# Second expert layer of a graph and mixture-of-experts kernel: groups of 128 tokens by unordered pairs of experts

## The chip, the cores and the metric

The kernel runs on one core of one Trainium2 chip. The metric is the device time in microseconds (us) of that core; the kernel before took 976.24 us, the median of three runs (975.2 to 976.76). A core has a matrix engine (PE, with its weight loads shown as PEld), VectorE (DVE), ScalarE (ACT), GpSimd (POOL) and SyncE (SP), each with a queue of its own, and 16 DMA engines that all of them share. Engines are ordered among each other by semaphores only.

## The reference, cut to what matters

128 graphs of 64 nodes with 128 features give 8192 tokens. The result is built in four residual steps: attention, experts, attention, experts.

```python
x = x + gnn0(layernorm(x), adj)
x = x + ffn0(layernorm(x))        # 8 experts, hidden width 512, best 2 of 8, weights renormalised
x = x + gnn1(layernorm(x), adj)
x = x + ffn1(layernorm(x))        # 8 experts, hidden width 256, best 2 of 8, weights = softmax values
```

Only ffn1 is touched in earnest. For each token with normalised row xf it is

```python
probs = softmax(xf @ gate_w + gate_b)
top2_vals, top2_idx = top_k(probs, 2)
out = sum over the two experts e of  val_e * (gelu(xf @ W1[e] + b1[e]) @ W2[e] + b2[e])
```

## The kernel before, in words

The program is five stages, one after the other, with all engines in each: blocks of layer 0 (attention and routing), groups of layer 0 (experts), blocks of layer 1, groups of layer 1, and a last stage that adds the results.

**Blocks.** `blocks(L)` takes 8 blocks of 1024 tokens, as 8 tiles of 128. Per block VectorE brings in the input (in layer 1 it adds the two expert results of layer 0, L932), takes statistics (L877), makes the masked scores, adds the attention to the input (`add_attention`, L984) into `x1w`, finds the two best experts (`route`) and computes for every token and expert the row in a sorted buffer (`places`, L1038 to L1053). PE does the transposes, the scores, features and attention, and the running counts (`ranks`, L535 to L540). PE's L506 writes half the partitions at a time with a 64-column weight tile; all its other operations use 128 by 128 tiles. POOL then scatters each token's row twice, once to each of its experts, into `row_buf` (L446): 16 indirect DMAs of 128 rows of 130 floats per block. SP stores the attention result with the two weights into `x1_buf` (L300).

A row is the normalised token as a high and a low half in f16, its token number and its expert's number. `row_buf` has a region for each expert; `pad_row` fills what isn't used, a fixed part of it in layer 0's blocks (L355) and the ends of the regions once the counts are known (L368).

**Groups.** `groups(L)` runs over 71 groups of 256 sorted rows, each of one expert (`NG = 16384 / 256 + 7`), in turns of 8. `group_tables` makes the list of the groups' experts and rows. SP loads the rows four groups ahead (L378). PE transposes them (L593), multiplies them by the first weights, three f16 products for each f32 one (`up`, L607), and after ACT's gelu, which adds the first bias, and VectorE's split into a high and a low half (L1184, L1188) by the second weights (`down`, L621). VectorE adds the second bias (L1201) and computes the destination (L1173, L1176, L1198), POOL scatters 2 times 128 result rows of 128 floats into `y_buf` (L454). On PE, group g's transposes come three groups ahead, its first product two groups ahead of its second one. PE reads the experts' numbers of a turn into registers at its start.

**The last stage.** SP loads `x1_buf` and both halves of `y_buf` back, VectorE adds the two weighted results to each token (L932, 128 instructions), SP writes the output (L429).

## Time and profile before

| what | value |
|---|---|
| median of three runs | 976.24 us |
| the profiled execution's own time | 975.38 us |
| its span, first to last instruction | 973.5 us |
| time around the span | 1.88 us |
| busy, share of the span: PE, PEld, DVE, ACT, POOL | 66%, 56%, 77%, 49%, 56% |
| granted clock of TensorE, mean over the span | 0.789 of 2.4 GHz |
| indirect DMAs of POOL | 256 into row_buf, 284 into y_buf |

Busy shares are means over five stages with different limits, so they name no bound by themselves. The stages are told apart by which lines run: layer 0's blocks to about 209 us, its groups from 244 to 470 us, layer 1's blocks to 702 us, its groups from 732 to 928 us, and the last stage to 973.5 us. An idle time in a row is the wait of that engine just before the instruction, with what ended it.

### The profile page before, as it was taken

Reading aid. Unit: us, or ns where it says so; the run is one execution under the profiler, and the core shown is the slowest. Engines: PE = TensorE matmul, PEld = TensorE weight load, DVE = VectorE, ACT = ScalarE, POOL = GpSimd, SP = SyncE. Lnnn points to the kernel's source line nnn. Section 1 sums busy time; section 2 is a strip of 40 time slices with the busy share of each in tenths; the row PEclk is TensorE's granted clock in tenths of the full one; section 3 lists DMA queues with packets and bytes.
Section 4 is the critical chain, followed back from the end, with each engine's and each line's share of the span. In section 5 each row is a group of like instructions: output and inputs, shape, how many; then the busy total and the mean of one; then the engine's idle time right before and its main releaser. Section 6 shows DMA issues by size and latency. Waiting matters only on the chain.

```text
span 973.5 us, 23618 instructions
## 1 busy us (share of the span) xinstructions
PE 641.5 (66%) x6081; PEld 547.3 (56%) x6082; DVE 752.1 (77%) x2881; ACT 480.3 (49%) x1065; POOL 545.7 (56%) x544
## 2 busy tenths in 40 slices
PE   3767667550999999999077768777207777777400
PEld 2656556450899999998056557655206655555300
DVE  6688898763699999999468989997526778787458
ACT  2365665420677777776046655665205655555100
POOL 0017677676276776767200665666763777777700
PEclk9875775755899999999557776777558999999655
DMA  8283333232233332326524454332333333333899
GB/s 221 61 199 107 112 93 95 69 107 77 71 88 89 88 87 82 86 82 176 140 57 120 137 146 136 88 88 66 94 90 87 105 98 102 94 104 97 226 233 285
DMA packets 168828, 111.51 MB, mean 115 GB/s; under 512 B 30306, under 2 KB 157737, under 8 KB 168776
## 3 DMA queue, kind: packets, MB, share of 16 engines
q1 hardware_dynamic: 151496, 77.04, 30.7%
q0 software_dynamic: 17280, 33.87, 10.4%
q8 instruction: 21, 0.34, 0.1%
q14 instruction: 31, 0.25, 0.1%
HBM read 60.32 MB, written 52.36 MB: 116 GB/s over the span
## 4 chain that ended last, share of the span: by engine, by line
PE 34%; DVE 22%; issue 19%; POOL 13%; DMA 5%; ACT 5%; SPq 1%; POOLq 1%; DVEq 0%; ACTq 0%
PE bank L607 10%; PE bank L621 9%; POOL row_buf L446 7%; POOL y_buf L454 5%; PE bank L509 4%; DVE xin L932 3%; PE bank L490 3%; DVE stat L877 3%; DVE x1w L984 3%; PE bank L506 2%; ACT xn L682 2%; PE bank L526 2%; PE bank L593 2%; DMA y_buf<-g_y,g_dst 2%; PE bank L513 2%
## 5 line engine op out<-in xcount | busy, mean ns | idle before, releaser
L446 POOL DMA_INDIRECT row_buf<-pay,slot x256 | 253.8, 992 | 245.0 <-DVE slot L1053 165.7
L454 POOL DMA_INDIRECT y_buf<-g_y,g_dst x284 | 291.6, 1027 | 137.0 <-issue 89.0
L607 PE MATMUL bank<-g_xT,w 128*128 128x256 f16 x1278 | 168.1, 278 | 0.9 <-ACT g_xT L786 0.3
L786 ACT ACTIVATE g_xT<-bank 128x512 f16<-128x512 f16 x142 | 84.8, 598 | 168.5 <-PE bank L593 164.4
L607 PEld LDWEIGHTS bank<-g_xT,w 128*128 x1278 | 118.3, 99 | 19.6 <-issue 2.1
L593 PE MATMUL bank<-ident,g_in 128*128 128x128 f16 x568 | 57.3, 225 | 83.6 <-DMA g_in<-row_buf 70.0
L793 ACT ACTIVATE xn<-bank,b_cols 128x256 f32<-128x256 f32 x216 | 86.8, 474 | 23.0 <-PE bank L607 15.9
L621 PE MATMUL bank<-w,g_h 128*128 x1260 | 84.4, 219 | 18.6 <-DVE g_y L1201 18.6
L793 ACT ACTIVATE xt<-bank,b_cols 128x256 f32<-128x256 f32 x210 | 84.5, 474 | 14.6 <-PE bank L607 11.4
L621 PEld LDWEIGHTS bank<-w,g_h 128*128 128x128 f16 x1260 | 76.0, 98 | 27.2 <-issue 25.1
L593 PEld LDWEIGHTS bank<-ident,g_in 128*128 128x128 f16 x568 | 37.0, 100 | 93.2 <-issue 73.9
L1173 DVE TENSOR_SCALAR g_k<-g_in,grp_e 128x2 f32<-128x2 f32 x142 | 34.1, 240 | 43.9 <-DMA g_in<-row_buf 36.0
L682 ACT ACTIVATE xn<-xin,nmr,rstd 128x128 f32<-128x128 f32 x128 | 50.8, 480 | 31.4 <-DVE nmr L921 31.4
L932 DVE SCALAR_TENSOR_TENSOR xin<-yin,xin 128x128 f32<-128x128 f32 x160 | 43.7, 345 | 26.7 <-DMA yin<-y_buf 24.2
L509 PEld LDWEIGHTS bank<-to_score,xnT 128*128 128x128 f32 x256 | 49.6, 289 | 22.3 <-issue 22.3
L490 PE MATMUL bank<-cst,xn 128*128 128x128 f32 x128 | 31.9, 412 | 44.1 <-ACT xn L682 41.4
L1201 DVE SCALAR_TENSOR_TENSOR g_y<-bank,b_bc 128x256 f32<-128x256 f32 x142 | 59.5, 419 | 0.0
L509 PE MATMUL bank<-to_score,xnT 128*128 128x64 f32 x256 | 55.1, 385 | 0.0
L526 PE MATMUL bank<-h_sb,pair_eT 128*128 128x137 f32 (+1 forms) x256 | 52.2, 384 | 2.4 <-ACT pair_eT L672 2.4
L526 PEld LDWEIGHTS bank<-h_sb,pair_eT 128*128 128x128 f32 x256 | 49.1, 288 | 6.4 <-issue 4.0
L1198 DVE CAST g_dst<-g_row 128x2 uint32<-128x2 f32 x142 | 25.9, 182 | 33.4 <-DMA y_buf<-g_y,g_dst 33.1
L490 PEld LDWEIGHTS bank<-cst,xn 128*128 128x128 f32 x128 | 22.4, 208 | 48.3 <-ACT xn L682 37.6
(182 smaller groups left out, 1333.7 us busy)
## 6 DMA issues: line engine op xcount, KB each, us to landing
g_in<-row_buf SPq DMA_DIRECT2D x142, 130.0 KB
yin<-y_buf SPq DMA_DIRECT2D x24, 512.0 KB, 6.2
x_buf<-x1w SPq DMA_DIRECT2D x16, 520.0 KB, 4.6
xin<-x_buf SPq DMA_DIRECT2D x10, 520.0 KB, 4.4
y_buf<-g_y,g_dst POOLq DMA_INDIRECT x284
xin<-in_x_dram SPq DMA_DIRECT2D x8, 512.0 KB, 4.2
adj_in<-in_adj_dram SPq DMA_DIRECT2D x16, 256.0 KB, 3.2
row_buf<-pay,slot POOLq DMA_INDIRECT x256, 2.4
```

The lines of the kernel that those rows point to most:

```text
L446: pool.indirect_dma_start(row_buf[L][:, :], bass.IndirectOffsetOnAxis(ap=slot[q][:, k, t:t + 1], axis=0), pay[q][:, t, :], None).then_inc( ...
L454: pool.indirect_dma_start(y_buf[L][:, :], bass.IndirectOffsetOnAxis(ap=g_dst[k][:, t:t + 1], axis=0), g_y[k][:, t, :], None, bounds_check= ...
L490: last = nc.tensor.transpose(bank[t // 4][:, (t % 4) * P:(t % 4 + 1) * P], src[:, t, :], ident)
L509: last = nc.tensor.matmul(bank[2][:, t * NODES:(t + 1) * NODES], xnT[:, t, :], to_score[:, 2 * L, :], start=False, stop=(t % 4 == 3), skip ...
L526: last = nc.tensor.matmul(att_tile[L][t], pair_eT[:, t, :], h_sb[:, t, H_AT:H_AT + att_w[L]], start=True, stop=True)
L593: last = nc.tensor.transpose(x_ps[q][:, hl, t * P:(t + 1) * P], rows16[:, t, hl * D:(hl + 1) * D], ident16[:, :])
L607: last = nc.tensor.matmul(dst, w[:, bass.ds(e * (2 * HID[L]) + (wp * HID[L] + c * P), P)], g_xT[q][:, xp, :], start=(m == 0), stop=(m == 2))
L621: last = nc.tensor.matmul(bank[5 + k % 2][:, t * D:(t + 1) * D], hid[:, hp, c, t * P:(t + 1) * P], w[:, bass.ds(e * (2 * HID[L]) + (2 * c ...
L682: last = nc.scalar.activation(dst[:, t, :], src[:, t, :], ACT.Identity, bias=nmr[:, t:t + 1], scale=rstd[:, t:t + 1])
L786: nc.scalar.activation(g_xT[q][:, :, :], x_ps[q], ACT.Copy).then_inc(s.gT_sb, 1)
L793: nc.scalar.activation(g_act[q][:, c, :], bank[2 * q + c // 2][:, (c % 2) * GRP:(c % 2 + 1) * GRP], ACT.Gelu, bias=b1_cols[L][:, bass.ds(e ...
L932: last = V.scalar_tensor_tensor(src[:, t, X_AT:X_END], y[k][:, t, :], src[:, t, k:k + 1], src[:, t, X_AT:X_END], ALU.mult, ALU.add)
```

## The change

Layer 1's experts are no longer taken one by one. There are 28 unordered pairs of experts; every token belongs to one pair.

- **Routing.** `route_pairs` makes a key from the two experts (a power of two for each, added) and compares it with the 28 keys; `ranks` and `places_pairs` count in 28 lists instead of 8. The weights are put in the pair's order. Each token is scattered once, as a row of 260 floats: the former 130, and beside them the attention result with its weights (`row0`, `row1` hold both side by side). Layer 1 has no store to an `x1_buf` any more; the reuse of `x1w` waits for the scatter of two blocks before instead.
- **Pads.** 128 pad rows of 260 floats ahead of each of the 28 lists are written once in layer 0's blocks. The last group of a list starts 128 rows before its end; rows that this takes twice get a destination out of bounds (`twice`). The writes to the ends of the regions are gone.
- **Tables.** `pair_tables` makes the pair's two experts, the first row and the count of rows taken twice for 91 groups (`NGP = 8192 / 128 + 27`) on partitions, and PE spreads them with one product. `pair_constants` prepares constants and bias rows on VectorE between `split_first(0)` and `groups(0)`.
- **Groups.** `pair_groups` runs over 91 groups of 128 rows, two experts each, in turns of 8, rows loaded eight groups ahead. PE does 2 transposes, 16 products in `up` (for each of 2 experts and 2 chunks three f16 products and one that adds the first bias) and 14 in `down` (for each expert one for the second bias and six). The bias products have 2 rows on the contracted side (`b1_row`, `sx_row`, `b2_row`, `sh_row` are tiles of 2 partitions), all others 128. ACT does one gelu over 512 columns and the high half after it, VectorE the low half and two multiply-adds with the token's weights, the second onto the attention result. POOL scatters 128 finished rows straight to the output.
- **The last stage** is gone, and with it the second `y_buf` and `x1_buf`.

The core of the diff:

```diff
+                def up(g, k, es):
+
+                    wait_past(pe, s.act_done, g - 3)
+                    pe.wait_ge(s.gT_sb, g + 1)
+                    w = w1[1][:, :, :, :].rearrange("p e a h -> p (e a h)")
+                    for m, e in enumerate(es):
+                        for c in range(NC[1]):
+                            dst = bank[k % 4][:, (m * NC[1] + c) * PG:(m * NC[1] + c + 1) * PG]
+                            for j, (wp, xp) in enumerate(((0, 0), (0, 1), (1, 0))):
+                                nc.tensor.matmul(dst, w[:, bass.ds(e * (2 * HID[1]) + (wp * HID[1] + c * P), P)],
+                                                 p_xT[k % 2][:, xp, :], start=(j == 0), stop=False)
+                            last = nc.tensor.matmul(dst, b1_row[:, bass.ds(e * HID[1] + c * P, P)], sx_row[:, :], start=False, stop=True)
+                    last.then_inc(s.h_ps, 1)
+
+                def down(g, k, es):
+                    w = w2[1][:, :, :, :, :].rearrange("p e c a d -> p (e c a d)")
+                    wait_past(pe, s.y_ready, g - 1)
+                    hid = p_h[k % AHEAD]
+                    pe.wait_ge(s.h_split, g + 1)
+                    for m, e in enumerate(es):
+                        dst = bank[5 + k % 2][:, m * D:(m + 1) * D]
+                        nc.tensor.matmul(dst, sh_row[:, :], b2_row[:, bass.ds(e * D, D)], start=True, stop=False)
+                        for c in range(NC[1]):
+                            for j, (wp, hp) in enumerate(((0, 0), (0, 1), (1, 0))):
+                                last = nc.tensor.matmul(dst, hid[:, hp, m * NC[1] + c, :],
+                                                        w[:, bass.ds(e * (2 * HID[1]) + (2 * c + wp) * D, D)],
+                                                        start=False, stop=(c == NC[1] - 1 and j == 2))
+                    last.then_inc(s.y_done, 1)
...
+                def gelu(g, k):
+                    wait_past(act, s.h_split, g - 1)
+                    act.wait_ge(s.h_ps, g + 1)
+                    nc.scalar.activation(p_act[k % 2], bank[k % 4][:, :].rearrange("p (c r) -> p c r", c=4),
+                                         ACT.Gelu, scale=1.0 / (S_X * S_W)).then_inc(s.act_done, 1)
+                    act.wait_ge(s.act_done, g + 1)
+                    nc.scalar.activation(p_h[k % AHEAD][:, 0, :, :], p_act[k % 2], ACT.Copy, scale=S_H).then_inc(s.hi_done, 1)
...
+                def split(g, k):
+
+                    dve.wait_ge(s.hi_done, g + 1)
+                    V.scalar_tensor_tensor(p_h[k % AHEAD][:, 1, :, :], p_act[k % 2], S_H, p_h[k % AHEAD][:, 0, :, :],
+                                           ALU.mult, ALU.subtract).then_inc(s.h_split, 1)
+
+                def finish(g, k, turn):
+
+                    rows, a = p_in[k], k % AHEAD
+                    wait_past(dve, s.y_out[a], 16 * (DEEP // AHEAD * turn + k // AHEAD))
+                    dve.wait_ge(s.g_loaded[k], 16 * (turn + 1))
+                    dve.wait_ge(s.y_done, g + 1)
+                    y = bank[5 + k % 2]
+                    ch.did(V.scalar_tensor_tensor(p_y[a], y[:, 0:D], rows[:, ROW_W:ROW_W + 1], rows[:, ROW_W + X_AT:WIDE_W], ALU.mult, ALU.add))
+                    V.tensor_tensor(p_dst[a][:, :], rows[:, D:D + 1], twice[:, bass.ds(g, 1)], ALU.add)
+                    ch.wait()
+                    V.scalar_tensor_tensor(p_out[a], y[:, D:2 * D], rows[:, ROW_W + 1:ROW_W + 2], p_y[a], ALU.mult, ALU.add).then_inc(s.y_ready, 1)
...
-                    for LL in range(2):
-                        sp.dma_start(row_buf[LL][NE * CAP:ROWS, :].rearrange("(t p) w -> p t w", p=P),
-                                     pad_row[:, :].unsqueeze(1).to_broadcast([P, SPARE // P, ROW_W])).then_inc(spare_out, 16)
+                    sp.dma_start(row_buf[0][NE * CAP:ROWS, :].rearrange("(t p) w -> p t w", p=P),
+                                 pad_row[:, 0:ROW_W].unsqueeze(1).to_broadcast([P, SPARE // P, ROW_W])).then_inc(spare_out, 16)
+                    sp.dma_start(row_buf[1].rearrange("(l c) w -> c l w", c=CAPP)[0:PG, :, :],
+                                 pad_row[:, :].unsqueeze(1).to_broadcast([P, PAIRS, WIDE_W])).then_inc(spare_out, 16)
...
-                wait_past(dve, s.stored[q], 16 * turn)
+                if L == 0:
+                    wait_past(dve, s.stored[q], 16 * turn)
+                else:
+                    wait_past(dve, s.scattered[q], 16 * TILES * turn)
```

## Rows read from the trace of the kernel before

**Rows 1.** Stages: stretch, length, busy us of each engine (instructions), clock, DMA share, GB/s

```profile
478.00:702.00 224.00, 150.87 (x896) 124.18 (x896) 186.12 (x875) 119.28 (x266) 108.75 (x110) 0.68 0.37 104
776.00:925.00 149.00, 104.13 (x1171) 79.47 (x1168) 108.75 (x323) 74.40 (x157) 114.27 (x115) 0.94 0.43 120
928.00:973.50 45.50, 0.00 (x0) 0.00 (x0) 34.50 (x128) 0.00 (x0) 0.00 (x0) 0.50 1.02 277
```

**Rows 2.** Timeline, groups of layer 1: start us, us, engine, line, operation, idle before

```profile
893.03 0.97 POOL L454 DMA_INDIRECT y_buf<-g_y,g_dst  x1 [0.30 <-issue]
```

**Rows 3.** Timeline, end of the last scatter of layer 1's groups

```profile
926.87 0.97 POOL L454 DMA_INDIRECT y_buf<-g_y,g_dst  x1 [0.30 <-issue]
```

**Rows 4.** Timeline, from layer 1's last slots to its first group result

```profile
702.14 0.17 DVE L1053 CAST slot<-slot_f 128x16 uint32<-128x16 f32 x1
...
726.96 0.95 POOL L446 DMA_INDIRECT row_buf<-pay,slot  x1 [0.30 <-issue]
...
732.28 0.23 DVE L1173 TENSOR_SCALAR g_k<-g_in,grp_e 128x2 f32<-128x2 f32 x1 [20.21 <-DMA g_in<-row_buf]
...
743.41 1.38 POOL L454 DMA_INDIRECT y_buf<-g_y,g_dst  x1 [15.50 <-DVE g_y L1201]
```

**Rows 5.** Timeline of PEld, one group of layer 0 and the next one's start

```profile
411.00 0.27 PEld L593 LDWEIGHTS bank<-ident,g_in 128*128 128x128 f16 x4
411.23 1.25 PEld L607 LDWEIGHTS bank<-g_xT,w 128*128 x12
412.48 1.44 PEld L621 LDWEIGHTS bank<-w,xtT 128*128 128x128 f16 x24
413.88 0.21 PEld L593 LDWEIGHTS bank<-ident,g_in 128*128 128x128 f16 x3
```

**Rows 6.** The chain in order of time, layer 0's groups: first product after a turn's start

```profile
372.60 1.41 PE bank L607 x12
...
396.73 1.45 PE bank L607 x12
```

**Rows 7.** Timeline of PE in layer 0's second block, with both weight tiles

```profile
45.62 1.51 PE L509 MATMUL bank<-to_score,xnT 128*128 128x64 f32 x8
47.06 0.65 PE L506 MATMUL bank<-xnT,to_score 128*64 128x256 f32 x4
47.64 1.10 PE L509 MATMUL bank<-to_score,xnT 128*128 128x64 f32 x8
48.59 2.18 PE L513 MATMUL bank<-w_feat,xnT 128*128 128x144 f32 x16
```

**Rows 8.** Groups of instructions: line, engine, shapes, count, busy us, mean ns

```profile
L621 PE MATMUL bank<-w,g_h 128*128 x1260 | 84.4, 219 | 18.6 <-DVE g_y L1201 18.6
L786 ACT ACTIVATE g_xT<-bank 128x512 f16<-128x512 f16 x142 | 84.8, 598 | 168.5 <-PE bank L593 164.4
L730 ACT ACTIVATE pay<-xt 128x1024 f16<-128x1024 f32 x16 | 16.9, 1055 | 0.3
L1188 DVE SCALAR_TENSOR_TENSOR g_h<-xn,g_h 128x512 f16<-128x512 f32 x54 | 36.4, 701 | 1.2
L984 DVE SCALAR_TENSOR_TENSOR x1w<-bank,rinv,xin 128x136 f32<-128x136 f32 x64 | 17.8, 352 | 0.8
```

**Rows 9.** Timeline of a layer 1 block: one step of the slot computation

```profile
636.41 0.21 DVE L1038 TENSOR_TENSOR pos<-bank,base_run 128x64 f32<-128x64 f32 x1
```

**Rows 10.** Timeline of SP's queue in layer 0's first blocks

```profile
43.86 8.70 SPq L355 DMA_DIRECT2D row_buf<-pad_row  x2
52.95 4.30 SPq L282 DMA_DIRECT2D adj_in<-in_adj_dram  x1
63.55 0.39 SPq L294 DMA_DIRECT2D xin<-in_x_dram  x1
```

**Rows 11.** Stretches of 1 us there, columns as in rows 1

```profile
60.00:61.00 1.00, 0.45 (x3) 0.24 (x2) 1.00 (x5) 1.00 (x4) 0.00 (x0) 0.92 1.23 225
...
63.00:64.00 1.00, 0.57 (x17) 0.57 (x18) 0.97 (x5) 0.00 (x0) 0.00 (x0) 0.78 0.02 4
```

**Rows 12.** Timeline, same stretch: VectorE's first score step after block 3's input is awaited

```profile
70.27 0.69 DVE L944 SCALAR_TENSOR_TENSOR e_act<-e_sb 128x512 f32<-128x512 f32 x1 [1.07 <-ACT e_sb L716]
```

More of the change, by code:

```diff
@@ L37 @@
 NO_TOKEN = 4 * N_TOK
+PAIRS = NE * (NE - 1) // 2
+PG = P
+NGP = N_TOK // PG + PAIRS - 1
+CAPP = N_TOK + PG
+WIDE_W = ROW_W + X_END
+FULL_W = ROW_W + TILE_W
+DEEP = 8
 AHEAD = 4
@@ new lines, in _ @@
+            blocks(0)
+            pe.wait_ge(stage_in, 32)
+            for e in range(NE):
+                for c in range(NC[0]):
+                    k = e * NC[0] + c
+                    last = nc.tensor.matmul(bank[0][:, k:k + 1], w_stage[:, e * HID[0] + c * P:e * HID[0] + (c + 1) * P],
+                                            vec_cols[:, V_B + e:V_B + e + 1], start=True, stop=True)
+            last.then_inc(bw_ps, 1)
+            groups(0)
+            blocks(1)
+            pair_groups()
@@ L819, in groups, with pair_groups, copy_x, turn @@
                 turn(TURNS, last=True)
-            for L in range(2):
-                blocks(L)
-                groups(L)
+            def pair_groups():
+                s = SL[1]
+                x_ps = [bank[b][:, 0:PG].bitcast(F16).rearrange("p (h n) -> p h n", h=2) for b in (4, 7)]
+                def copy_x(g, q):
+                    act.wait_ge(s.gT_ps, g + 1)
+                    nc.scalar.activation(p_xT[q], x_ps[q], ACT.Copy).then_inc(s.gT_sb, 1)
+                def gelu(g, k):
[5 more added lines that the diff above has]
+                    nc.scalar.activation(p_h[k % AHEAD][:, 0, :, :], p_act[k % 2], ACT.Copy, scale=S_H).then_inc(s.hi_done, 1)
+                load_table(ACT.Gelu)
+                act.wait_ge(s.tables, 1)
+                for k in range(2):
+                    copy_x(k, k)
+                gelu(0, 0)
+                copy_x(2, 0)
+                gelu(1, 1)
+                def turn(i, last=False):
+                    n = PAIR_TAIL - 2 if last else DEEP
+                    for k in range(n):
+                        if not last or k < n - 1:
+                            copy_x(DEEP * i + k + 3, (k + 1) % 2)
+                        gelu(DEEP * i + k + 2, k + 2)
+                with act.Fori(0, PAIR_TURNS) as i:
+                    turn(i)
+                turn(PAIR_TURNS, last=True)
+            blocks(0)
+            groups(0)
+            blocks(1)
+            pair_groups()
         @block.vector
```

432 lines of the change are left out of this document (306 added, 126 removed).

## The prediction, made before the change was run

> **What bounds the kernel now.** I read the stages first, then within the two stages that change most the timeline, then the chain for the pace of a full PE. In layer 1's groups POOL is busy 114.27 of 149 us, more than any other engine [rows 1], and its scatters follow each other with only 0.30 us between them, ended by nothing but their own issue [rows 2]: 115 in 149 us is 1.30 us each, two for a group, 2.59 us a group. That stage is bound by the number of indirect DMAs. The last stage has no PE, ACT or POOL at all, DMA at a share of 1.02, and takes 45.5 us [rows 1]. Between the stages, layer 1's last slots are ready at 702.31, but POOL still scatters until 727.91 and the first group's rows arrive at 732.28 [rows 4]. So three costs hang on layer 1's scatters and results. The blocks of layer 1 are led by VectorE, 186 of 224 us [rows 1], and POOL is no limit there.
>
> **The last stage goes.** The sum starts from the end of the last scatter, 927.84 [rows 3]. After the change an output row is final when it lands. I keep 3.7 us from the start of the last scatter to the end: 0.97 for the scatter [rows 2] and an estimated 2.7 for landing and the last wait, from the 4.37 us that stand between the last row scatter's end and the first loaded data, a landing and a load together [rows 4].
>
> **Scatters of the last block.** 8 in place of 16, and none of block 6 left over. From 702.31, 0.8 to start, 8 x (0.96 + 0.30) = 10.1, and the 4.37 us of before to the first data [rows 4]: 717.6 in place of 732.28, a gain of 14.7. The rows are 1040 bytes instead of 520; no row shows an indirect DMA of that width. It costs between 0.96 us (the price goes by row) and 1.92 (by byte); the scatters of 512 and 520 bytes are alike, so I take 0.96, with +7.7 here at the upper bound. The tables and the weight split on VectorE, 12 us before and some 11 after, end at 713, still covered by the scatters. In the blocks VectorE now waits for the scatter of two blocks before ahead of writing `x1w`; the rest of its own block is queued behind that wait, and PE and ACT behind it. 10.1 us of scatters in some 24 us a block leave it idle; at the upper bound, 17.8 and a landing, it would cost about 2 us in each of 7 blocks.
>
> **Work added in layer 1's blocks.** Steps over 224 instead of 64 elements: 64 cost 0.21 us [rows 9], 512 cost 0.70 [rows 8], so 224 cost about 0.38. In `places_pairs` two such steps in place of one of 64 and two of 64, a longer reduction and two small steps, in `route_pairs` one against one of 64: +0.6 us a block, in part hidden in the pauses of the statistics chain beside which they run. PE's counts get 3.5 times the columns, perhaps 0.3 us. I take +4 for 8 blocks, bounds 0 and +9.
>
> **Pads.** SP's pads are now 0.93 + 3.73 MB instead of 1.86 MB. Before, the queue was full: the next load, `adj`, took 4.30 us to issue, where others take 0.39 [rows 10]. The backlog was gone by 63 us, at 225 GB/s [rows 11]; VectorE waits for block 3's input at about 69, just ahead of the row at 70.27 [rows 12], and that input is issued at 63.55. The added 2.8 MB at 225 GB/s are 12.5 us: the queue is free at 75.5, the input lands at 78 to 79, so +8. Bounds: 0, if wide rows go much faster or loads pass them, and +14. `pair_constants` costs nothing: VectorE and PE idle before the first group of layer 0, and it has some 15 us there for an estimated 10.
>
> So the first data of the pair groups come at 717.6 + 4 + 8 = 729.6. From there to the first scatter it was 11.1 us before [rows 4]; the groups are half as long, I take 9.
>
> **The price of a pair group, and where I chose.** In layer 0's groups PE is full: 4 transposes in 0.23 us, 12 products of 256 columns in 1.25, 24 of 128 in 1.40 [rows 5], so 58 ns for any with 128 columns. A turn of 8 groups takes 24.13 us where 8 x 2.88 are 23.0: 1.1 us for a turn's start with its 10 register loads [rows 6]. The pair group has 2 + 16 + 14 = 32 products of 128 columns, 1.87 us, and its turn has 20 loads: 1.1 to 2.3 us in 8 groups, 0.2 a group. That gives 2.07 us. The other engines are below it: ACT copies 256 columns, does a gelu and a high half of 512 each (0.60 for 512, 1.055 for 1024 [rows 8], so 0.37 + 0.69 + 0.62, less overlap: 1.6); VectorE 0.70 + two of 0.35 + waits = 1.5 [rows 8]; POOL 1.27 [rows 2].
>
> But six of these products contract over 2 rows, and the tile of the array follows the operand's size: L506, with 64 weight columns, runs as 128*64. A tile of another shape isn't fed while the last one is in flight. L509 ends by the profile at 45.62 + 1.51 = 47.13 and L506 starts at 47.06; L506 ends at 47.71, L509 starts at 47.64. From L509 to L513, where the tile stays, the next product starts at 48.59, 0.15 before the end at 48.74 [rows 7]. So a switch means: start 0.07 us before the modelled end of the one before. A 128-column f16 product lasts 219 ns [rows 8]; after a switch the next starts 0.15 us later, and with an estimated 0.02 for its weights 0.17, not 0.058: 0.11 a switch. In program order a group is 2 transposes, four times (three products, one bias product), then twice (one bias product, six products). `up`'s last bias product and `down`'s first stand side by side, so `up` has 7 switches and `down` 3: ten, 1.10 us, 3.17 us a group. Bounds: none of it, if a tile of 2 rows counts as a full one; 0.09 a switch (start exactly at 0.15) and a short turn's start 2.91; 0.14, if the product waits half of its 0.104 us weight load (1.25 us for 12 [rows 5]), and a long turn's start 3.56.
>
> The Trainium skill states this for every shape: "Changing tiling mode (not just tile) drains the TensorE" (TensorEngine Tiling (Array Packing), Key Properties). The trace agrees for 64 columns; no row here shows it for few rows.
>
> **Sum.** 729.6 + 9 + 90 x 3.17 + 3.7 = 1027.6 us of span; with the 1.88 us around it 1029.5. The profiled execution took 975.38, 0.9 below the median of 976.24; I don't correct for so little. Forecast 1029 us, 5.5% slower. Its own range: 2.91 us a group, no pads and nothing added in the blocks, 994; 3.56 with both at their upper bounds, 1075.
>
> **The rivals.**
> - *No price for the switches* (faster): the 2-row tile runs in the full array. 729.6 + 9 + 90 x 2.07 + 3.7 + 1.88 = 930.5 us, 905 to 950. For it: no row shows a tile of few rows. Against it: the 64-column tile, at both halves of the partitions, is named and waited for as one of its own.
> - The Trainium skill's page TensorE: Matmul & The Clock Gate ("Why this matters for your kernels") says of a single product that K=32 takes the same time as K=128; taken as the whole price, that is this rival. It says nothing of the switch.
> - *ACT or the turn's start as the bound*, without switches: gelu, wait and high half stand in one chain with the copy; without overlap and with 0.2 for each of three waits ACT needs 2.3 us a group: 951.
> - *Only the prefetch of the weights is lost*: half a weight load, 0.05 a switch, 2.57 us a group, 975.5, no change.
> - *Wide scatters priced by byte*: +21 us on either side, 951 or 1050.
>
> The point from which the sign turns: (973.5 - 742.3) / 90 = 2.57 us a group, that is 0.05 us a switch. The gain without switches is 45 us; ten switches waited out cost twice that.
>
> **How the numbers follow.** Switches waited out 0.48, the same with dear scatters 0.03, prefetch lost 0.08 (of it 0.03 within 0.2%, 0.03 slower, 0.02 faster); free switches 0.27, with ACT or turns as the bound 0.09, with dear scatters 0.05. Slower by over 0.2% 0.54, the same 0.03, faster 0.43; 0.2% is about what a measurement of this kernel can tell from no change. Both signs are likely, so the range takes in both: 915 to 1070, which leaves out a tenth at either end.
>
> **What would show it.** A tile other than 128*128 in the rows of the bias products, and PEld idle before and after each; a pair group of 2.9 to 3.6 us with PE busy throughout and POOL mostly idle. With 2.0 to 2.1 us and gapless weight loads the switch step is wrong. Block 3's input on VectorE should show an idle of about 8 us near 70 us; none refutes the pads' term. The last block's scatters should take 10 us, and the first group's data follow 15 us after the last slots. What makes the prediction wrong above all is the reading of a tile's shape from one line's 64 columns.

## The result and the profile after

The changed kernel takes 1174.37 us (median of four, 1171.64 to 1179.31), the kernel before on the same chip 975.72 (975.14 to 976.76): a ratio of 1.204, with a 95% interval of 1.200 to 1.208. The forecast was 1029. The profiled execution took 1171.64 us, its span is 1169.8, the granted clock 0.673 of 2.4 GHz in the mean (0.789 before). On the page of the changed kernel, in slices of 29 us:

```profile
PE   4656673459999997377688643999999999999996
...
POOL 0057777727777767002223322111121112111211
PEclk9777756579999999567766855555555555555555
```

From the 26th slice on PE is full and POOL, the bound of this stage before [rows 1], is a tenth to a fifth busy. The clock is at 0.5, that is 1.2 GHz, from the 24th slice on, where the last block leaves PE three to four tenths busy, and stays there to the end. The stages by stretches (us, busy us of PE, PEld, DVE, ACT, POOL, then clock, DMA share, GB/s), beside [rows 1]:

```profile
702.00:717.00 15.00, 1.58 (x2) 0.50 (x2) 9.94 (x43) 0.00 (x0) 8.07 (x8) 0.50 0.20 72
717.00:735.00 18.00, 13.05 (x86) 7.42 (x87) 2.74 (x6) 5.48 (x11) 0.41 (x1) 0.50 0.23 60
735.00:1160.00 425.00, 401.81 (x2828) 251.48 (x2826) 119.46 (x358) 140.84 (x262) 86.91 (x90) 0.50 0.13 36
```

The last stage of before, 45.5 us, is gone; the groups' stage took 183.5 us before between the starts of its first and last scatter and takes 425.8 now. The start of a pair group in the timeline of PE:

```profile
1041.27 0.42 PE L712 MATMUL bank<-ident,yin 128*128 128x128 f16 x2
1041.48 0.53 PE L727 MATMUL bank<-g_xT,w 128*128 128x128 f16 x3
1041.94 0.28 PE L729 MATMUL bank<-sx_row,b_row 2*128 2x128 f16 x1
1042.15 0.50 PE L727 MATMUL bank<-g_xT,w 128*128 128x128 f16 x3
1042.59 0.28 PE L729 MATMUL bank<-sx_row,b_row 2*128 2x128 f16 x1
```

The bias product's tile is called 2*128, another one than its neighbours' 128*128, and the timeline of PEld shows the pause on both sides of it:

```profile
953.87 0.10 PEld L729 LDWEIGHTS bank<-sx_row,b_row 2*128 x1 [0.20 <-issue]
954.08 0.23 PEld L727 LDWEIGHTS bank<-g_xT,w 128*128 x3
954.52 0.10 PEld L729 LDWEIGHTS bank<-sx_row,b_row 2*128 x1 [0.20 <-issue]
```

The group's two transposes, with no switch between them or behind them, take from 1041.27 to 1041.48, 0.21 us: 0.107 us a product, where 0.058 was counted. From a bias product's weights to the next product's it is 953.87 to 954.08, some 0.21 us, 0.11 more than 0.107: the price of a switch as forecast. The groups start every 4.51 us (L712 at 1041.27, 1045.78, 1050.29 and 1054.81), and 32 x 0.107 + 10 x 0.11 = 4.52.

The ends of the sum, in the timelines of VectorE, POOL, PE (its wait for the first rows) and POOL again, and the last piece of POOL's queue (count, then min/median/max in ns):

```profile
703.41 0.17 DVE L1263 CAST slot<-slot_f 128x8 uint32<-128x8 f32 x1
```

```profile
704.39 0.95 POOL L487 DMA_INDIRECT row_buf<-row,slot  x1 [8.80 <-DVE slot L1263]
...
713.56 1.03 POOL L487 DMA_INDIRECT row_buf<-row,slot  x1 [0.30 <-issue]
```

```profile
719.17 0.37 PE L712 MATMUL bank<-ident,yin 128*128 128x128 f16 x2 [10.30 <-DMA yin<-row_buf]
```

```profile
734.59 0.98 POOL L501 DMA_INDIRECT out_dram<-g_y,p_dst  x1 [19.99 <-DVE g_y L1512]
...
1160.41 0.97 POOL L501 DMA_INDIRECT out_dram<-g_y,p_dst  x1 [0.96 <-DVE g_y L1512]
```

```profile
L139 POOLq DRAIN  x1: 9360/9360/9360, 1160.2 to 1160.2; - x1
```

So the miss, term by term against the forecast span of 1027.6: the first data at 719.2 and not 729.6, -10.4; from there to the first scatter 15.4 and not 9, +6.4; 90 group intervals of (1160.41 - 734.59) / 90 = 4.73 and not 3.17, +140.5; from the last scatter's start to the end 9.4 and not 3.7, +5.7. That is 1169.8. The question for the experiments was the 140: why 0.107 us a product and not 0.058.

### The profile page after: what moved, and what is told of

It reads as the page before. It is cut to its first block, busy times and chain, and to the rows that moved or that the text cites. A ratio compares the mean times of both kernels' runs of the same rounds, so it can differ in the third digit from the quotient of the medians.

```text
span 1169.8 us, 27438 instructions
## 1 busy us (share of the span) xinstructions
PE 917.2 (78%) x7433; PEld 700.6 (60%) x7434; DVE 710.9 (61%) x2735; ACT 526.2 (45%) x1125; POOL 434.5 (37%) x429
## 4 chain that ended last, share of the span: by engine, by line
PE 60%; DVE 20%; issue 8%; POOL 5%; ACT 3%; DMA 2%; SPq 1%; POOLq 0%; DVEq 0%; ACTq 0%
PE bank L727 13%; PE bank L742 12%; PE bank L655 8%; PE bank L669 7%; PE bank L729 7%; POOL row_buf L487 4%; DVE stat L1036 3%; DVE row L1172 3%; PE bank L739 3%; DVE xin L1117 2%; PE bank L556 2%; PE bank L712 2%; PE bank L537 2%; PE bank L641 1%; PE bank L553 1%
## 5 line engine op out<-in xcount | busy, mean ns | idle before, releaser
L487 POOL DMA_INDIRECT row_buf<-row,slot x192 | 194.2, 1012 | 292.1 <-DVE slot L1263 165.5
L501 POOL DMA_INDIRECT out_dram<-g_y,p_dst x91 | 88.3, 970 | 358.5 <-DVE g_y L1512 338.0
L727 PE MATMUL bank<-g_xT,w 128*128 128x128 f16 x1092 | 184.0, 307 | 0.9 <-ACT g_xT L947 0.9
L496 POOL DMA_INDIRECT y_buf<-g_y,g_dst x142 | 151.7, 1069 | 76.1 <-issue 46.8
L727 PEld LDWEIGHTS bank<-g_xT,w 128*128 x1092 | 95.7, 128 | 35.6 <-issue 3.4
L655 PE MATMUL bank<-g_xT,w 128*128 128x256 f16 x852 | 106.0, 275 | 0.4 <-issue 0.3
L729 PE MATMUL bank<-sx_row,b_row 2*128 2x128 f16 x364 | 102.9, 283 | 0.0
L655 PEld LDWEIGHTS bank<-g_xT,w 128*128 x852 | 80.3, 98 | 10.4 <-issue 1.0
L906 ACT ACTIVATE g_xT<-bank 128x512 f16<-128x512 f16 x71 | 42.4, 597 | 85.2 <-PE bank L641 84.3
L729 PEld LDWEIGHTS bank<-sx_row,b_row 2*128 x364 | 35.8, 98 | 71.3 <-issue 71.2
L742 PE MATMUL bank<-w,g_h 128*128 x540 | 73.7, 310 | 0.0
L712 PE MATMUL bank<-ident,yin 128*128 128x128 f16 x182 | 37.9, 312 | 34.0 <-issue 22.9
L742 PEld LDWEIGHTS bank<-w,g_h 128*128 128x128 f16 x540 | 50.0, 137 | 14.1 <-issue 8.7
```

The lines of the kernel that those rows point to most:

```text
L487: pool.indirect_dma_start(row_buf[L][:, :], bass.IndirectOffsetOnAxis(ap=slot[q][:, k, t:t + 1], axis=0), pay[q][:, t, :] if L == 0 else r ...
L496: pool.indirect_dma_start(y_buf[:, :], bass.IndirectOffsetOnAxis(ap=g_dst[k][:, t:t + 1], axis=0), g_y[k][:, t, :], None, bounds_check=TOP ...
L501: pool.indirect_dma_start(out[:, :], bass.IndirectOffsetOnAxis(ap=p_dst[k][:, 0:1], axis=0), p_out[k], None, bounds_check=N_TOK - 1, oob_i ...
L655: last = nc.tensor.matmul(dst, w[:, bass.ds(e * (2 * HID[L]) + (wp * HID[L] + c * P), P)], g_xT[q][:, xp, :], start=(m == 0), stop=(m == 2))
L712: last = nc.tensor.transpose(x_ps[k % 2][:, hl, :], rows16[:, hl * D:(hl + 1) * D], ident16[:, :])
L727: nc.tensor.matmul(dst, w[:, bass.ds(e * (2 * HID[1]) + (wp * HID[1] + c * P), P)], p_xT[k % 2][:, xp, :], start=(j == 0), stop=False)
```

## The experiments

Three theories stood at the start: S, the ten switches a group cost 0.11 us each and also hold the clock down; R, products with only two active rows hold it down; C, a stream of 128-column products can't keep the high clock, or can't run at 0.058 us, for another reason.

### Tiles with more rows

`full_rows` gives the bias products' operands all 128 rows, zero below the first two; `rows64` does it with 64.

```diff
-        b1_row = sb("b1_row", [2, NE * HID[1]], F16)
-        b2_row = sb("b2_row", [2, NE * D], F16)
-        sx_row, sh_row = sb("sx_row", [2, P], F16), sb("sh_row", [2, P], F16)
+        b1_row = sb("b1_row", [P, NE * HID[1]], F16)
+        b2_row = sb("b2_row", [P, NE * D], F16)
+        sx_row, sh_row = sb("sx_row", [P, P], F16), sb("sh_row", [P, P], F16)
...
+            V.memset(b1_row[:, :], 0.0)
+            V.memset(b2_row[:, :], 0.0)
```

> Only change: the four tiles of the bias products have 128 partitions, 126 of them zero in the bias rows, so every product contracts over 128 rows; same count of products. Theory S (switches of the array's tile cost 0.11 us each and by their number hold the clock at 1.2 GHz): rows show 128*128 throughout, no idle before a bias product, clock 1.0, a group 32 x 0.058 + 0.3 for the turn = 2.2 us, about 935 us. Theory R (products with few active rows hold the clock down, whatever the switches): the same 935. Theory C (the stream of a pair group can't hold 2.4 GHz for another reason): the switches' 1.1 us a group go, the clock stays 1.2, 32 x 0.107 + 0.3 = 3.7 us a group, about 1075 us.

> As the changed kernel, but the bias tiles have 64 partitions (62 of the bias rows zero): ten switches a group, another tile shape, 32 times as many active rows. S: as the changed kernel, 1174 us, clock 1.2, tile 64*128 in the rows. R: more active rows bring the clock back: 1.87 + 1.1 + 0.3 = 3.3 us a group, about 1035 us. C: 1174.

`full_rows` took 1055.95 us, a ratio of 1.082 (1.079 to 1.085). A group in the timeline of PE:

```profile
853.68 0.27 PE L712 MATMUL bank<-ident,yin 128*128 128x128 f16 x2
853.84 0.35 PE L727 MATMUL bank<-g_xT,w 128*128 128x128 f16 x3
854.10 0.23 PE L729 MATMUL bank<-sx_row,b_row 128*128 128x128 f16 x1
854.23 0.35 PE L727 MATMUL bank<-g_xT,w 128*128 128x128 f16 x3
...
856.57 0.27 PE L712 MATMUL bank<-ident,yin 128*128 128x128 f16 x2
```

The tile is 128*128 everywhere, the clock in the stage is back (0.85 to 0.96 in stretches of 40 us, where it was 0.50), and the run is 118 us shorter. But it is 120 us longer than S had it. Four products take 0.37 to 0.39 us, 0.09 to 0.10 each at the high clock, and a group 2.88 us. S explains the clock, not the pace. `rows64` ran twice, 1177.5 us (the traced run, clock 0.50 throughout the pair stage, groups 4.55 us apart) and 1157.3, on both sides of the change's 1174: half the rows active, the switches as before. R had it at 1035 and falls with it.

### The biases side by side, and no biases

`grouped` keeps the two rows and moves the products: all twelve of `up`, then its four biases, then the two of `down`, then its twelve. So a group has two switches. In this order the products don't add up to the change's sums, so the kernel serves for its time alone. `no_bias` leaves both biases of layer 1's experts out of the computation: 26 products, no switch.

> Same six bias products over 2 rows, but the four of the first stage stand after its 12 others and the two of the second ahead of its 12: 2 switches a group in place of 10. S: clock 1.0, 1.87 + 0.22 + 0.3 = 2.4 us a group, about 955 us. R: clock 1.2 GHz, 3.42 + 0.22 + 0.3 = 3.9 us a group, about 1095 us. C: the same 1095.

> Leaves out both biases of the second expert layer: the six bias products of a group are gone, 26 are left, no switch. S and R: clock 1.0, 26 x 0.058 + 0.3 = 1.8 us a group, where ACT's chain of about 1.7 comes close, about 900 us. C: clock 1.2, 3.1 us a group, about 1020 us. Against full_rows it gives the price of six products over 128 rows: 32 us, or less if ACT or a turn's start bounds.

`grouped` took 1056.13 us, a ratio of 1.082 (1.080 to 1.084), clock 0.83 to 0.91 in the stage: with six two-row products in every group the clock is high, which is the second witness against R. S had this run at 955 us: the clock is as S has it, the pace again isn't. `no_bias` took 986.29, where 900 was expected, a ratio of 1.010 (1.008 to 1.012); a group of 26 products takes 2.11 us, 0.081 each. So even without biases and switches the stream of products is dearer than 0.058, and C lives on for the pace. Two things in the traces had not been read before the prediction. One is the start of a turn, in PE's timeline of `no_bias`:

```profile
790.31 1.01 PE L740 MATMUL bank<-w,g_h 128*128 x12
795.53 0.39 PE L712 MATMUL bank<-ident,yin 128*128 128x128 f16 x2 [4.20 <-issue]
795.84 1.46 PE L727 MATMUL bank<-g_xT,w 128*128 128x128 f16 x12
797.09 1.49 PE L740 MATMUL bank<-w,xnT 128*128 x12
798.37 0.42 PE L712 MATMUL bank<-ident,yin 128*128 128x128 f16 x2
798.59 1.40 PE L727 MATMUL bank<-g_xT,w 128*128 128x128 f16 x12
799.82 0.83 PE L740 MATMUL bank<-w,xtT 128*128 x12
800.49 0.27 PE L712 MATMUL bank<-ident,yin 128*128 128x128 f16 x2
800.60 0.83 PE L727 MATMUL bank<-g_xT,w 128*128 128x128 f16 x12
801.36 1.01 PE L740 MATMUL bank<-w,g_h 128*128 x12
```

PE stands still for 4.2 us at every turn, comes back at the low clock, then does twelve products from 800.60 to 801.36, 0.063 each, and from the next groups on falls back to 0.081. The reading that the experiments below bear out: in the slow stretch after the stop PE's queue gets ahead of PE, and the pace lasts as long as that lead. The other is in the instructions of PE's own queue, of which `full_rows` has in its up products, its biases and the loads (engine, kind, count, then min/median/max in ns):

```profile
L727 PEldq FUSED_REGOPS  x112: 46/46/46, 800.9 to 849.2; - x112
```

```profile
L742 PEldq ALU_OP  x85: 32/32/32, 800.0 to 840.2; - x85
```

```profile
L307 PEldq TENSOR_LOAD <-pair_tab x26: 544/1157/2417, 724.7 to 1036.5; - x26
```

Over 50 us with 14 groups L727 has 112 register operations, 8 a group; L729 has 4, L739 2, L742 8, six of 32 and two of 46 ns: 22 a group, one for each new weight address that depends on the expert. C got a name: Q, PE's queue sets the pace, and each run-time address costs its operation beside a product of 128 columns.

### Fixed addresses

`static_full` is `full_rows` with the weights of experts 0 and 1 for every group, `static_after` is the change itself with them. The choice of the experts is left out on PE.

```diff
                 def experts(g, n):
-                    return [table_values(mybir.EngineType.PE, pair_tab[0:1, k, :], g, n, NE - 1) for k in range(2)]
+                    return [[k] * n for k in range(2)]
```

> The bias tiles have 128 rows as in the run with full rows, and PE takes the weights of experts 0 and 1 for every pair group, at fixed addresses: the choice of the experts is left out on PE, and with it the register operations ahead of the products (22 a group of 46 ns in the trace of the full-rows run) and the loads of registers at each turn's start (4.2 us for 8 groups). Theory Q (PE's own instruction queue sets the pace: each run-time address costs its 46 ns beside the product's 58): a group takes 32 x 0.058 = 1.9 us in place of 2.88, and no 4.2 us at the turns: 1056 - 91 x 0.95 - 12 x 4.2 = 920 us, with 915 to 950 by what is late next. Rival C (a 128-column product that changes its weights takes 0.09 us by itself when the rows are full): only the turns' starts go, 1005 us, group 2.85 us.

> The changed kernel with its two-row bias tiles and ten switches a group, but experts 0 and 1 at fixed addresses (the choice is left out on PE). Theory S (the switches hold the clock at 1.2 GHz): clock 0.50 in the pair stage and a group of 32 x 0.107 + 10 x 0.11 = 4.5 us as before, since a register operation of 46 ns hides behind a product of 107; only the turns' starts of 2.2 us go: 1174 - 26 = 1148 us. Rival (the clock falls because register operations and switches together starve PE): clock back to 1.0 and a group of 1.87 + 1.10 = 2.97 us: 1015 us.

`static_full` took 904.75 us, a ratio of 0.927 (0.925 to 0.928). A stretch of its stage (columns as above), and one of its groups:

```profile
780.00:820.00 40.00, 40.00 (x720) 40.00 (x718) 30.03 (x91) 33.63 (x68) 24.63 (x23) 1.00 0.36 104
```

```profile
830.25 0.27 PE L712 MATMUL bank<-ident,yin 128*128 128x128 f16 x2
830.36 0.33 PE L727 MATMUL bank<-g_xT,w 128*128 128x128 f16 x3
...
832.03 0.28 PE L712 MATMUL bank<-ident,yin 128*128 128x128 f16 x2
```

PE and PEld have no pause, the clock is 1.00, a group takes 1.79 us for 32 products, 0.056 each. Q holds and C in its first form falls: a 128-column product is not dear, its address is. Nor is a product with a run-time address slow in PE itself: in `no_bias`, with its 16 operations a group, the transposes of two groups start at 779.33 and 780.78, 1.45 us for 26 products, 0.056 each, in the stretch behind a turn's start. What PE's queue issues late, and not what PE does, sets the pace. Register loads and addresses together are 151 us of `full_rows`' 1056: 91 x (2.88 - 1.79) = 99 and some 11 turns with 4.2 us and the slow products behind.

`static_after` took 1148.99 us, 1.177 (1.175 to 1.180), the clock 0.50 through the whole stage and its groups 4.51 us apart. So ten switches hold the clock down by themselves, with no address operation and no stop at the turns in the stream, and at 0.107 us a product those operations cost nothing.

A kernel meant to keep the loads and drop the addresses (`loads_full`) came out without the loads, since nothing used them: its trace has no TENSOR_LOAD of the pair table, its 903.04 us repeat `static_full`, and the two prices were not told apart in this way.

> As static_full, but PE still loads the two experts of each group into registers at every turn's start and doesn't use them. Theory Q: products at 0.058 and 4.2 us a turn: about 920 + 50 = 970 us. Rival C: 1055 us, no different from the run with full rows. The difference to static_full is the price of the loads: 50 us by the 4.2 us seen at each turn.

### How many switches

`up_full` gives 128 rows to the first bias only (four switches a group), `down_full` to the second only (eight). `static_four` and `static_eight` are the same two with fixed addresses, the choice left out as above.

> The first bias's tile has 128 rows, the second bias's two: four tile switches a group in place of ten. Theory S (it is the number of switches that holds the clock; two a group let it rise in the grouped run, ten hold it down): I can't say on which side four fall. At the high clock a group takes 2.88 + 4 x 0.11 = 3.3 us and the run 1056 + 40 = 1096 us; at the low one 32 x 0.107 + 0.44 = 3.9 us and 1174 - 91 x 6 x 0.11 = 1114 us. The granted clock in the pair stage tells which (0.8 to 1.0, or 0.50).

> The other way round: the first bias's tile has two rows and the second's 128, so eight switches a group. Theory S: like ten, clock 0.50 in the pair stage, 32 x 0.107 + 8 x 0.11 = 4.3 us a group and 1174 - 91 x 2 x 0.11 = 1154 us. If the clock came back, 2.88 + 0.88 = 3.76 us a group and 1136 us.

> The kernel with the first bias's tile of 128 rows and the second's of two (four switches a group), experts 0 and 1 at fixed addresses: the choice of the experts is left out on PE. With the register operations present four switches cost nothing (1057 beside 1056 us). If they were hidden behind those operations, here, where PE takes 1.79 us a group with nothing between the products, each must show its 0.11 us: 1.79 + 0.44 = 2.23 us a group, 905 + 40 = 945 us. Rival (four switches are free whatever stands beside them): 905 us. If the clock falls instead, 32 x 0.107 + 0.44 = 3.9 us a group and 1095 us.

> The same with eight switches a group (the first bias in two rows, the second in 128), fixed addresses. With the register operations present the clock was high in part of the stage (0.54 to 0.91 in stretches of 40 us). Theory S (the number of switches a group decides, the operations have no part): a mix again, between the sum at the high clock, 1.79 + 0.88 = 2.67 us a group or 985 us, and the one at the low clock, 4.3 us a group or 1133 us; near the high end if operations and switches together had starved PE, at the low end if the switches alone do, as the run with ten and fixed addresses showed.

| kernel | switches | addresses | us | ratio (95%) | a group, us | clock in 40-us stretches, 740 to 940 |
|---|---|---|---|---|---|---|
| `static_full` | 0 | fixed | 904.75 | 0.927 (0.925 to 0.928) | 1.79 | 1.00 |
| `static_four` | 4 | fixed | 941.4 | 0.962 (0.959 to 0.964) | 2.20 | 1.00 |
| `static_eight` | 8 | fixed | 984.69 | 1.009 (1.006 to 1.013) | 2.61 | 0.95 to 1.00 |
| `static_after` | 10 | fixed | 1148.99 | 1.177 (1.175 to 1.180) | 4.51 | 0.50 |
| `full_rows` | 0 | run-time | 1055.95 | 1.082 (1.079 to 1.085) | 2.88 | 0.85 to 0.96 |
| `up_full` | 4 | run-time | 1057.29 | 1.083 (1.078 to 1.089) | 2.87 | 0.83 to 0.96 |
| `down_full` | 8 | run-time | 1087.41 | 1.114 (1.109 to 1.119) | 2.61 to 2.9, or 4.29 | 0.54 to 0.91 |
| the change | 10 | run-time | 1174.37 | 1.204 (1.200 to 1.208) | 4.51 | 0.50 |

With fixed addresses each switch shows its price at the high clock: (2.20 - 1.79) / 4 = 0.103 and (2.61 - 1.79) / 8 = 0.103 us. 941 and 985 were expected at 945 and 985. With run-time addresses four switches are free: `up_full` was expected at 1096 us and takes 1057, as `full_rows` does. The queue's pace, 2.88 us a group, and the products with their switches, 1.79 + 4 x 0.103 = 2.20, run beside each other, and the longer one counts. At the high clock even eight switches (2.61) stay below the queue's 2.88, and groups behind a turn's start, where the queue has a lead, come at exactly that 2.61. Three groups' starts in `down_full`, with all its run-time addresses:

```profile
804.54 0.27 PE L712 MATMUL bank<-ident,yin 128*128 128x128 f16 x2
807.15 0.28 PE L712 MATMUL bank<-ident,yin 128*128 128x128 f16 x2
809.96 0.28 PE L712 MATMUL bank<-ident,yin 128*128 128x128 f16 x2
```

The first two are 2.61 us apart, and the next interval, 2.81, is already the queue's. Three products behind a switch in the timeline of `static_eight`, where nothing but the switch stands between them:

```profile
845.31 0.33 PE L727 MATMUL bank<-g_xT,w 128*128 128x128 f16 x3
845.58 0.22 PE L729 MATMUL bank<-sx_row,b_row 2*128 2x128 f16 x1
845.73 0.34 PE L727 MATMUL bank<-g_xT,w 128*128 128x128 f16 x3
846.00 0.22 PE L729 MATMUL bank<-sx_row,b_row 2*128 2x128 f16 x1
```

From 845.31 to 845.58 it is 3 x 0.056 + 0.10, and from 845.58 to 845.73 0.056 + 0.10. The bias product itself lasts 0.22 us with 2 rows as with 128 (`static_full`'s L729, 0.22). The Trainium skill, on its page TensorE: Matmul & The Clock Gate ("Why this matters for your kernels"), says that a single product over 32 rows takes the same time as one over 128; for 2 rows and 128 the trace agrees by these two durations. Each switch around it, which that section doesn't speak of, costs nearly twice the 0.056 us of a product.

Between eight and ten switches the clock makes a step: at one clock the two differ by 0.21 us a group, as run with fixed addresses by 164 us. The stretches of the two, from 780 to 820:

```profile
780.00:820.00 40.00, 40.00 (x491) 29.45 (x488) 20.37 (x61) 23.18 (x47) 15.37 (x16) 1.00 0.25 70
```

```profile
780.00:820.00 40.00, 40.00 (x284) 25.24 (x283) 12.14 (x36) 13.93 (x27) 8.70 (x9) 0.50 0.13 37
```

Both stages begin at 0.50, the clock since about 685 us, and PE has next to nothing to do from 702 to 717 (2.8 us of 15). With eight switches and no stops the clock rises at 744 and stays up; with ten it never does. `down_full` has the same eight switches with run-time addresses, and its clock goes up and down within the stage:

```profile
742.00:759.00 17.00, 15.81 (x181) 11.49 (x179) 7.70 (x24) 8.84 (x17) 5.83 (x6) 1.00 0.22 63
759.00:780.00 21.00, 18.31 (x137) 12.79 (x137) 5.43 (x18) 6.82 (x13) 3.89 (x4) 0.51 0.13 39
```

Every fall within the stage comes 1 to 4 us after the beginning of a stop at a turn's start, where PE stands still for some 4 us (here from 757.8). The clock of `full_rows`, without switches, falls behind the same stops and stays at 0.50 for 3 to 7 us; that of `down_full` stays there for 7 to 55 us, at 4.29 us a group, as in `static_eight` at that clock. By these records it is the stops at the turns that let the clock fall, and the switches that put off its return; the address operations show no part of their own in it. 30 of the 90 intervals of `down_full` are 4.2 to 4.4 us long and 20 are 2.61; that is where its 31 us over `full_rows` lie. Expected were 1154 us, or 1136 with the clock back.

### The price of an address, and a way round it

Four kernels that compute all that the change computes, with no switches. `lean_full` keeps 512 times the expert's number in the table, reads both experts with one load, and puts both biases in one tile of that stride. `lean_bytes` has byte offsets in the table and slices the weights as bytes. `lean_wide` is `lean_bytes` with one edit more, and `wide_elem` is `lean_full` with that edit; here its part on PE, without the bias product, which moves behind the four others, and without the two operations more on VectorE:

```diff
                         for c in range(NC[1]):
-                            for j, (wp, hp) in enumerate(((0, 0), (0, 1), (1, 0))):
-                                last = nc.tensor.matmul(dst, hid[:, hp, m * NC[1] + c, :],
-                                                        w[:, bass.ds(e + (2 * c + wp) * D, D)],
-                                                        start=False, stop=(c == NC[1] - 1 and j == 2))
+                            for hp, n in ((0, 2 * D), (1, D)):
+                                nc.tensor.matmul(dst[:, 0:n], hid[:, hp, m * NC[1] + c, :],
+                                                 w[:, bass.ds(e + 2 * c * D, n)],
+                                                 start=(c == 0 and hp == 0), stop=False, skip_group_check=True)
```

> Nothing is left out: bias tiles of 128 rows, the table holds 512 times the expert's number, both experts' rows are read by one load, and the two biases lie in one tile with the same stride of 512. So the first address of each expert needs no operation and the others one addition of 32 ns: 14 a group in place of 22 of 46 ns. Theory Q: a group 2.88 - (22 x 0.046 - 14 x 0.032) = 2.31 us, and about 1 to 2 us less at each turn's start: 1056 - 52 - 12 to 24 = 980 to 992 us. Rival C: 1032 to 1044 us, from the turns' starts alone.

> As lean_full, whose operations had stayed at 22 a group (8 + 4 + 2 + 8 in its trace, so that its 2.80 us a group fit 1.79 + 22 x 0.046), but the table holds byte offsets and PE slices the weights as bytes, so that an address is the register itself (6 of the 22) or one addition (16 of 32 ns). Nothing is left out. Theory Q: a group 1.79 + 16 x 0.032 = 2.3 us, with lean_full's 1021 the sum 1021 - 91 x 0.5 = 976 us; if each address still takes an operation, of 32 ns, 1.79 + 22 x 0.032 = 2.5 us and 994 us. Rival (what counts is that the address is in a register at all, not the operation): 1021 us.

> lean_bytes, and in the second product the high and low half of the weights are one moving operand of 256 columns (their sum is left to two more VectorE operations of 0.35 us a group). Nothing is left out. Per group 28 products in place of 32, the same columns, and 18 addresses in place of 22, of which four stand before a product of 256 columns that takes 0.104 us and so hides its own operation. Theory Q: 10 to 14 visible additions of 32 ns beside 1.79 us, 2.1 to 2.25 us a group: 958 to 970 us, or 985 if the addresses at constant 0 still take an operation. Rival: VectorE, with 1.34 us of work a group before and 2.05 with the two operations and their chained waits, becomes the bound at 2.3 to 2.4 us a group: 976 to 985 us.

> Nothing is left out: lean_full (1021 us, operations of 46 and 32 ns) with the one edit of lean_wide (in the second product the weights' high and low half are one moving operand of 256 columns, so 18 addresses and 28 products in place of 22 and 32). Between lean_bytes and lean_wide that edit brought 43 us, 0.24 us for each expert of a group. Theory Q (an address costs PE its operation only beside a product of 128 columns): the same here, 1021 - 43 = 978 us. Rival (the 43 us came from the 85 to 96 ns operations of the byte addresses alone): 1010 us or more. Second rival (VectorE's two operations bound it at 2.4 us a group): 985 us.

| kernel | operations a group, ns (from the trace) | their sum, us | a group | over the products alone | us | ratio (95%) |
|---|---|---|---|---|---|---|
| `no_bias` | 10 x 46, 6 x 32 | 0.65 | 2.11 | 0.65 | 986.29 | 1.010 (1.008 to 1.012) |
| `full_rows` | 16 x 46, 6 x 32 | 0.93 | 2.88 | 1.09 | 1055.95 | 1.082 (1.079 to 1.085) |
| `lean_full` | 10 x 46, 12 x 32 | 0.84 | 2.81 | 1.02 | 1021.4 | 1.048 (1.046 to 1.050) |
| `lean_bytes` | 10 x 92, 12 x 32 | 1.30 | 3.17 | 1.38 | 1064.9 | 1.091 (1.088 to 1.095) |
| `lean_wide` | 9 x 92, 9 x 32 | 1.12 | 2.73 | 0.97 | 1021.7 | 1.047 (1.044 to 1.050) |
| `wide_elem` | 9 x 46, 9 x 32 | 0.70 | 2.37 | 0.61 | 983.24 | 1.006 (1.004 to 1.008) |

The products alone are 0.056 us for each of 128 columns and 0.104 for each of the wide ones. The expectation for `lean_full` was too low by 30 us, since an address at constant 0 still has its operation: 22 remained. Of its 35 us under `full_rows` 91 x 0.07 = 6 come from shorter operations and most of the rest from the turns, where PE stands 1.8 to 1.9 us in place of 4.2. `lean_bytes` made things worse, 1065 us where 976 to 994 were expected, for a reason its trace names:

```profile
L732 PEldq FUSED_REGOPS  x111: 85/92/102, 799.9 to 849.8; - x111
```

A byte slice seen as 16-bit values takes 92 ns of operations where the element slice takes 46, for eight addresses in `up` and two in `down`. Ten times 46 ns more than `lean_full` are 0.46 us, and the group is 0.36 us longer, 3.17 for 2.81: longer operations make a longer group, with nothing else changed on PE. Over the six kernels the excess over the products follows the operations' sum to within 0.2 us, on either side of it; in `full_rows` it is 1.09 / 22 = 0.05 us an address, a little more than the operation itself.

The wide operand takes 43 us off `lean_bytes` and 38 off `lean_full`: 978 was expected of `wide_elem`, 983.24 measured; of `lean_wide` 958 to 985, with 1021.7 measured, since it was reckoned without the 92 ns. Its second product and the bias product:

```profile
849.89 0.49 PE L744 MATMUL bank<-w,xtT 128*128 x4
850.22 0.22 PE L747 MATMUL bank<-b_row 128*128 x1
850.27 0.49 PE L744 MATMUL bank<-w,xtT 128*128 x4
```

An expert's five products take 849.89 to 850.27, 0.38 us, which is their columns and nothing else: two of 0.104 and three of 0.056 are 0.38. So the operations are hidden here, behind the products of 256 columns; the 0.6 us of the group over its products stand in `up`. VectorE has 31 of 40 us to do there and is near to being the next bound. No version that computes everything beat the kernel before; this one is 0.6% behind it.

## Why the prediction was wrong, point by point

- *The price of a pair group* is the step that failed, in its first term: 32 products at "58 ns for any with 128 columns" [rows 5], 1.87 us, are 32 x 0.107 = 3.42 us in the changed kernel. That is +1.55 of the 1.56 us by which a group's interval of 4.73 exceeds the forecast 3.17. The 58 ns were carried over without asking what the rows depend on. They hold at the high clock and where PE's queue keeps up. Layer 0's groups have 16 address operations for 12 products of 256 and 24 of 128 columns, the pair group has 22 for 32 of 128. At the high clock with run-time addresses 32 products take 2.88 us, not 1.87, and at that pace a few switches are free: the two terms don't add.
- *The clock* was not in the sum at all, a term put at nothing without a reason. The switches of [rows 7] at 47.06 and 47.64 lie in a stretch at a clock of 1.00; no question was asked what 0.11 us of standing still before and after every bias product would do to the clock of a stage. The switches and the low clock that comes with them are worth 118 us, `full_rows` against the change, and the range's upper end of 3.56 us a group had no term that could reach 4.73.
- *The sign and the switch* were right: the two-row tile is one of its own, ten switches are waited for, PE is full and POOL idle. The switch, 0.11 us with bounds of 0.09 and 0.14, measured 0.103 at the high clock and 0.11 at the low one; the 0.02 us for the weights in it was an estimate that no row showed, and from start to start across a switch it is 0.16 us at the high clock, not 0.17. "No price for the switches" is refuted by `static_four` and `static_eight`. But the forecast added 10 x 0.11 to a pace that doesn't exist in this kernel: with the clock up and the queue at 2.88 us, the ten switches would make 1.79 + 1.03 = 2.82 us of work beside it and, by this sum, cost nothing. They cost what they do because the clock is low. And with no switch at all the kernel is still slower than before, 1056 us in `full_rows`, so the sign was in part luck.
- *The turn's start*, 0.14 to 0.29 us a group: 0.32 in the changed kernel (38.6 us for 8 groups, 2.2 us of it standing still), 0.6 in `full_rows` (27.9 us for 8 groups, 4.2 of it standing still). That the stop is shorter at the low clock because the queue has a longer lead there is a reading, not tested.
- *Free switches, 930.5 us*: with full tiles and fixed addresses 905, with run-time addresses 1056. The rival would have been wrong with any tile, by the same failed step. So would have the break-even: at 2.57 us a group even `full_rows` (2.88) is on its far side, and the 0.05 us a switch had no meaning.
- *Pads*: +8 forecast. VectorE waits 3.0 us for block 3's input, ahead of this row:

```profile
71.43 0.69 DVE L1129 SCALAR_TENSOR_TENSOR e_act<-e_sb 128x512 f32<-128x512 f32 x1 [3.01 <-DMA xin<-in_x_dram]
```

  The row came at 70.27 before [rows 12], so the pads put it off by 1.2 us. Together with *the work added in the blocks* (+4) they should have made 12 us; the last slots are ready at 703.58 in place of 702.31, 1.3 us later, near the lower bounds of both. Block 3's input was issued at 62.77, before the 63.55 of [rows 10], and the DMA engines moved 286 to 338 GB/s from 56 to 72 us, where the sum went by the 225 of [rows 11].
- *Scatters of the last block*: 10.1 us forecast, 704.39 to 714.59 measured. The 64 scatters of 1040-byte rows have a mean of 0.99 us, as the 128 of layer 1 before with 520 bytes: priced by row, not by byte. From the last slots to the first data it is 15.6 us, where this step had 15.3.
- *To the first scatter* 9 us, measured 15.4: products at half the pace, and PE does `up` of three groups before the first `down`. *The end* 3.7 us from the last scatter's start, measured 9.4: the landing takes 2.1 of it, and what lasts to the end is the last instruction of POOL's queue, the DRAIN shown above, 9.36 us from 1160.18 to 1169.54. Before, the same instruction took 5.7 us from 924.98 and was hidden under the last stage. It was not in the sum. `full_rows`, `static_full` and `wide_elem` end 9.4 us behind their last scatter's start too.

## What to carry to other kernels

Before pricing a stream of short products by the product's duration, count what else its queue must issue for each: an address that hangs on a run-time value costs an operation of 32 to 46 ns, about 0.05 us a piece here, which a 256-column product hides, and a 128-column one at the low clock, but not a 128-column one at the high clock. The queue's time and the products' time run beside each other, so compare the two and don't add them. A small extra product with another tile shape costs two switches of 0.10 us, far more than itself, where PE sets the pace; where it must be there, fill its operand with zeros to the neighbours' tile. (Putting such products side by side brought `grouped` the time of `full_rows`, but an order that also keeps the sums right was not run.) And ask of every stop-and-go that a change brings into TensorE's stream what it does to the granted clock of the whole stage, since that is paid by all other products too.

## What the runs showed of the hardware that was not expected

- Ten tile switches a group of 32 products keep TensorE at 1.2 GHz through the 425 us from 735 to 1160 with PE busy in 95% of them, and in `static_after` with PE busy throughout; eight let it rise to 2.4 GHz with fixed addresses, and only part of the time where PE also stops for 4 us at each turn. What exactly decides is left open; that it is the switches and not the number of active rows is shown by `rows64` and `grouped`.
- A tile switch costs 0.103 us beside 0.056 us for a 128-column product at 2.4 GHz, and 0.11 beside 0.107 at 1.2 GHz.
- One load of 20 values into PE's registers goes with 1.8 us of idle PE at a turn's start, two loads of 10 with 4.2: it goes by load more than by value.
- Indirect rows of 1040 bytes cost the same 0.99 us per 128 as rows of 520.
- A kernel that ends with POOL's indirect DMAs also waits for the DRAIN of POOL's queue: 9.4 us from the last scatter's start, 7.3 of them after it has landed.
